# Contexts of a head in two groups of four key blocks, with a ring of six probability rows

## The reference

```
q, k, v = xh @ Wq + bq, xh @ Wk + bk, xh @ Wv + bv     # per head, xh = norm(x) as (b, s, 8, 16)
p = positions @ Wp
content = einsum('bqhd,bkhd->bhqk', q + u_bias, k)
pos_score = rel_shift(einsum('bqhd,khd->bhqk', q + v_bias, p))
attn = softmax((content + pos_score) / sqrt(128), axis=-1)
ctx = einsum('bhqk,bkhd->bqhd', attn, v)               # the "contexts" below
x = x + ctx @ Wo + bo
x = x + experts(norm(x))                               # router, top 2 of 8, gated up and down
```

## Time and profile before

| | us |
|---|---|
| median of 3 runs | 1645.3 |
| profiled execution | 1643.7 |
| its span, first to last instruction | 1641.8 |
| PE busy | 1517.0 (92%) |
| DVE busy | 1348.0 (82%) |
| ACT busy | 1094.1 (67%) |
| POOL busy | 1061.9 (65%) |

### The profile page before, as it was taken

The page is one execution under the profiler, slowest core; times in us unless marked ns, Lnnn a source line. Parts: engine busy times, 40 slices in busy tenths (PEclk is TensorE's granted clock), DMA queues, the critical chain, the costliest instruction groups (busy, mean ns, idle before and its releaser), DMA issues. The chain is left out here.

```text
span 1641.8 us, 49022 instructions
## 1 busy us (share of the span) xinstructions
PE 1517.0 (92%) x12235; PEld 1167.6 (71%) x12236; DVE 1348.0 (82%) x5147; ACT 1094.1 (67%) x2267; POOL 1061.9 (65%) x2019
## 2 busy tenths in 40 slices
PE   4799999999999999999999999999940899999997
PEld 2566676677667767767766776766530899999997
DVE  6689899889989988998898998878633688878886
ACT  3167777777777777677777777756720677777775
POOL 3177667667776766776676676655754376666766
PEclk8599999999999999999999999999975899999999
DMA  6836445544643653453364355333053244334443
GB/s 167 235 92 179 123 135 153 147 114 108 201 111 106 174 155 95 129 172 110 111 192 133 107 161 166 94 77 100 27 165 108 45 56 56 53 54 56 54 57 45
DMA packets 129820, 189.79 MB, mean 116 GB/s; under 512 B 20184, under 2 KB 93272, under 8 KB 129616
## 3 DMA queue, kind: packets, MB, share of 16 engines
q1 hardware_dynamic: 104048, 167.23, 37.2%
q0 software_dynamic: 25568, 20.14, 7.9%
HBM read 104.04 MB, written 69.96 MB: 106 GB/s over the span
## 5 line engine op out<-in xcount | busy, mean ns | idle before, releaser
L1122 DVE CUSTOM_DVE_ANT_0 junk<-pA,lmask 128x512 bf16<-128x512 f32 x1024 | 668.0, 683 | 85.0 <-PE pA L685 66.3
L1017 ACT ACTIVATE prob<-pB 128x512 f32<-128x512 f32 x384 | 229.9, 599 | 181.4 <-PE pB L704 98.5
L1653 POOL DMA_INDIRECT out<-yb,dst x142 | 231.6, 1631 | 129.6 <-ACT yb L1731 72.9
L683 PE MATMUL pA<-K,QL 96*128 96x512 f32 (+3 forms) x768 | 274.9, 359 | 12.4 <-DMA K<-split_operands 9.6
L706 PE MATMUL pB<-QL,K 97*128 97x512 f32 (+3 forms) x768 | 285.1, 372 | 1.4 <-ACT upper_diag L1017 1.2
L704 PE MATMUL pB<-QU,K 97*128 97x512 f32 (+3 forms) x640 | 265.9, 416 | 3.0 <-ACT prob L1017 1.9
L1019 ACT ACTIVATE prob<-pB 128x512 f32<-128x512 f32 x384 | 228.3, 594 | 15.1 <-PE pB L706 4.7
L685 PE MATMUL pA<-K,QU 96*128 96x512 f32 (+3 forms) x640 | 226.2, 354 | 1.2 <-DVE acc L1122 0.2
L722 PE MATMUL pC<-prob,vext 128*17 128x256 f32 x3088 | 217.0, 384 | 0.3 <-POOL prob L597 0.3
L597 POOL TENSOR_TENSOR prob<-prob,upper_diag 128x128 f32<-128x128 f32 x384 | 184.6, 481 | 32.0
L704 PEld LDWEIGHTS pB<-QU,K 97*128 97x128 f32 x640 | 120.9, 189 | 112.6 <-issue 61.8
(11 more groups left out here) (308 smaller groups left out, 3482.7 us busy)
## 6 DMA issues: line engine op xcount, KB each, us to landing
QL<-split_operands SPq DMA_DIRECT2D x64, 256.0 KB, 3.5
QU<-split_operands SPq DMA_DIRECT2D x64, 256.0 KB, 4.0
K<-split_operands SPq DMA_DIRECT2D x64, 256.0 KB, 4.3
xg<-routed_rows SPq DMA_DIRECT2D x75, 132.0 KB, 2.7
split_operands<-c_h SPq DMA_DIRECT2D x32, 256.0 KB, 5.3
split_operands<-c_l SPq DMA_DIRECT2D x32, 256.0 KB, 5.5
QL<-split_operands SPq DMA_DIRECT2D x64, 128.0 KB, 3.4
QU<-split_operands SPq DMA_DIRECT2D x64, 128.0 KB, 3.9
```

The lines of the kernel that those rows point to most:

```text
L683: mm = pe.matmul(dst[:, 0:low], QL[0:KROWS, s, q], K[0:KROWS, s, k0:k0 + low], start=True, stop=True)
L1017: act.activation(p[:, 0:HALF], pB[:, 0:HALF], ACT.Exp, scale=SCALE).then_inc(p_exp, 1)
L1122: v.tensor_tensor_reduce(out, src[:, :], lmask[:, at:at + HALF], 1.0, -3.0e38, ALU.add, ALU.max, acc[:, s, qb, n % 2:n % 2 + 1]).then_inc( ...
L1653: po.indirect_dma_start(dram["out"], bass.IndirectOffsetOnAxis(dst[k][:, a:a + 1], 0), yb[k][:, a, :], None, compute_op=ALU.add).then_inc( ...
```

## The change

The contexts of a head go in two groups of four instead of four groups of two: kb 4 to 7 of the head before in unit 1, kb 0 to 3 in unit 6. A row is so held longer, and the ring has six rows; since 8 rows a head don't divide by 6, a table FROM gives each head's first row. LATE, the count with which `pv_done` and `p_mask` start, goes from 2 to 4, and ACT waits on `pv_done` in steps of a group. The memory of the two added rows comes from the operand parts: gl now uses c's buffer. Therefore the stores of c have a semaphore of their own, `c_stored`, and from the second batch on ACT waits for them ahead of writing gl's high part (h = 3, u = 6). For the first batch gl's parts lie in rows 4 and 5 of the ring. GpSimd clears four rows ahead of the loop and not three. At the end of the last batch four contexts are left and not two.

```diff
-RING = 4
-LATE = 2
+RING = 6
+LATE = 4
-        parts = {... for n in ("c", "k", "gl", "gu")}
+        parts = {... for n in ("c", "k", "gu")}
+        parts["gl"] = parts["c"]
+        FROM = (4, 0, 2, 5, 2, 4, 0, 2)
+        def probs(h, kb):
+            return prob[(FROM[h % H] + kb % RING) % RING]
+        early_gl = (prob[4][:, :].bitcast(F32R), prob[5][:, :].bitcast(F32R))
-        PAIRS_AT = {1: (-1, 6), 4: (0, 0), 6: (0, 2), 8: (0, 4)}
+        GROUPS_AT = {1: (-1, 4), 6: (0, 0)}
-                            sp.dma_start(stored_to(...), stored_from(name, low, side)).then_inc(stored, 16)
+                            sp.dma_start(stored_to(...), stored_from(name, low, side)).then_inc(c_stored if name == "c" else stored, 16)
                             sp.wait_ge(stored, in_dram)
+                            sp.wait_ge(c_stored, c_in_dram)
-            for i in range(1, RING):
+            for i in range(4):
                 po.memset(prob[i][:, :], 1.0).then_inc(set_pool, 1)
-                        if u in PAIRS_AT:
-                            back, kb = PAIRS_AT[u]
-                            context(b, h + back, kb)
-                            context(b, h + back, kb + 1)
+                        if u in GROUPS_AT:
+                            back, from_kb = GROUPS_AT[u]
+                            for kb in range(from_kb, from_kb + NB // 2):
+                                context(b, h + back, kb)
+                if name == "gl" and half == 0 and not isinstance(nb, int):
+                    act.wait_ge(c_stored, nb * C_N)
-                            act.wait_ge(pv_done, b * (H * NB) + h * NB + u)
+                            act.wait_ge(pv_done, b * (H * NB) + h * NB + (LATE if u == 1 else 2 * LATE if u <= RING else 3 * LATE))
```

More of the change, by code:

```diff
@@ L105, in attention_phase @@
         xn = sb("xn", [P, NB, E])
-        parts = {n: (sb(n + "_h", [P, S], F32R), sb(n + "_l", [P, S], F32R)) for n in ("c", "k", "gl", "gu")}
+        parts = {n: (sb(n + "_h", [P, S], F32R), sb(n + "_l", [P, S], F32R)) for n in ("c", "k", "gu")}
+        parts["gl"] = parts["c"]
         QL, QU, K = keep["stacks"]
@@ L166, in attention_phase @@
         upper, swapped = sem("upper_form_ready"), sem("r_swapped")
-        stk, stored = [sem(f"stk{i}") for i in range(SLOTS)], sem("operands_stored")
+        stk, stored, c_stored = [sem(f"stk{i}") for i in range(SLOTS)], sem("operands_stored"), sem("content_operands_stored")
         d_r, d_big, set_r = sem("router_in"), sem("experts_in"), sem("set_router")
@@ L249, in attention_phase @@
         PLACES = {"c": ((0, 0), (1, 0)), "k": ((2, 0),), "gl": ((0, 1),), "gu": ((1, 1),)}
-        ST_N = 16 * 4 * sum(len(p) for p in PLACES.values())
+        ST_N, C_N = 16 * 4 * sum(len(p) for p in PLACES.values()), 16 * 4 * len(PLACES["c"])
         STORE_AT = {2: ("c",), 3: ("k",), 4: ("gl", "gu")}
         READY = {"c": 2, "k": 4, "gl": 7, "gu": 8}
-        PAIRS_AT = {1: (-1, 6), 4: (0, 0), 6: (0, 2), 8: (0, 4)}
+        GROUPS_AT = {1: (-1, 4), 6: (0, 0)}
         FOUR, SIDE = H // 2, P // 2
@@ L259, in stored_to, with stored_from @@
             return dram["operands"][bass.ds(nb % 2, 1), op, FOUR * side:FOUR * side + FOUR, 2 * low + row, :, :].rearrange("o h d s -> (o d) h s")
-        def stored_from(name, low, side):
-            return parts[name][low][SIDE * side:SIDE * side + SIDE, :].bitcast(F32)
-        DVE_SET, DVE_BIAS, POOL_SET = 14, 12, 15
+        def stored_from(name, low, side, early=False):
+            return (early_gl if early and name == "gl" else parts[name])[low][SIDE * side:SIDE * side + SIDE, :].bitcast(F32)
+        DVE_SET, DVE_BIAS, POOL_SET = 14, 12, 16
         D_W, D_CST = 16 * 8, 16 * 5
@@ L325, in store @@
                         for side in range(2):
-                            sp.dma_start(stored_to(nb, op, low, row, side), stored_from(name, low, side)).then_inc(stored, 16)
+                            sp.dma_start(stored_to(nb, op, low, row, side), stored_from(name, low, side)).then_inc(c_stored if name == "c" else stored, 16)
             def store_side(name, side):
@@ L330, in store_side @@
                     for low in range(2):
-                        sp.dma_start(stored_to(0, op, low, row, side), stored_from(name, low, side)).then_inc(first_stored[side], 16)
+                        sp.dma_start(stored_to(0, op, low, row, side), stored_from(name, low, side, True)).then_inc(first_stored[side], 16)
             sp.sem_inc(d_x2, 16)
@@ L368, in batch @@
                         sp.dma_start(xt[:, :, :], dram["x"][bass.ds((b + 2) % B, 1)].rearrange("o (t p) e -> p (o t) e", p=P)).then_inc(d_x, 16)
-                    through, in_dram = known(sp, HPB * (b * (H * S2U) + h * S2U) + 1), known(sp, (b + 1) * ST_N)
+                    through, in_dram, c_in_dram = (known(sp, n) for n in (HPB * (b * (H * S2U) + h * S2U) + 1, (b + 1) * (ST_N - C_N), (b + 1) * C_N))
                     sp.wait_ge(set_dve, DVE_SET)
@@ L419, in _ @@
                 sp.wait_ge(mrow_in[i], 4 * B * 32)
-            sp.wait_ge(stored, (B - 1) * ST_N)
+            sp.wait_ge(stored, (B - 1) * (ST_N - C_N))
+            sp.wait_ge(c_stored, (B - 1) * C_N)
             sp.wait_ge(swapped, B * 64)
@@ L451, in _ @@
             po.memset(vext[:, :, :, :], 0.0).then_inc(set_pool, 1)
-            for i in range(1, RING):
+            for i in range(4):
                 po.memset(prob[i][:, :], 1.0).then_inc(set_pool, 1)
             po.memset(mhalf[:, :], -0.5).then_inc(set_pool, 1)
-            po.wait_ge(set_pool, 9)
+            po.wait_ge(set_pool, 10)
             po.affine_select(out=ident[:, :], in_=ident[:, :], compare_op=ALU.not_equal, fill=1.0, base=0,
@@ L589, in batch @@
                             if kb > 0:
-                                po.memset(prob[kb % RING][0:1, P * kb - 1:P * kb], 0.0)
-                            p = prob[kb % RING][:, P * kb:P * kb + P]
+                                po.memset(probs(h, kb)[0:1, P * kb - 1:P * kb], 0.0)
+                            p = probs(h, kb)[:, P * kb:P * kb + P]
                             po.affine_select(out=p, in_=p, compare_op=ALU.is_ge, fill=0.0, base=0,
@@ L721, in context @@
                 for strip in range(STRIPS):
-                    mm = pe.matmul(pC[VW * strip:VW * strip + D + 1, :], vext[:, kb, h % H, :], prob[kb % RING][:, quarter * strip:quarter * strip + quarter],
+                    mm = pe.matmul(pC[VW * strip:VW * strip + D + 1, :], vext[:, kb, h % H, :], probs(h, kb)[:, quarter * strip:quarter * strip + quarter],
                                    start=(kb == 0), stop=(kb == NB - 1), skip_group_check=True)
@@ L937, in high @@
                 cut = slice(HALF * half, HALF * half + HALF)
-                act.activation(parts[name][0][:, cut], src[:, cut], ACT.Copy).then_inc(hi_done, 1)
+                if name == "gl" and half == 0 and not isinstance(nb, int):
+                    act.wait_ge(c_stored, nb * C_N)
+                dst = early_gl if name == "gl" and isinstance(nb, int) else parts[name]
+                act.activation(dst[0][:, cut], src[:, cut], ACT.Copy).then_inc(hi_done, 1)
             def upper_high(nb, half, src):
@@ L1106, in low @@
                 v.wait_ge(hi_done, nb * HI_N + n + 1)
-                v.tensor_tensor(parts[name][1][:, cut], src, parts[name][0][:, cut].bitcast(F32), ALU.subtract).then_inc(low_done, 1)
+                high, dst = early_gl if name == "gl" and isinstance(nb, int) else parts[name]
+                v.tensor_tensor(dst[:, cut], src, high[:, cut].bitcast(F32), ALU.subtract).then_inc(low_done, 1)
             def super_out(src, done):
```

2 lines of the change are left out of this document (1 added, 1 removed).

## The result

The changed kernel takes 1715.37 us (median of 4 runs, 1714.85 to 1715.67) against 1643.97 (1641.35 to 1646.98) of the kernel before in the same comparison: a ratio of 1.0425, 95% interval 1.0396 to 1.0453. Forecast were 1656 us, range 1630 to 1682. The direction was right, the size was not, and the range didn't hold it.

What follows compares the result with a forecast made beforehand. Three close limits: PE in units 1, 4, 6, 8, the PE-ACT round trip elsewhere, and DVE. Per head -0.23 + 0.35 + 0.05 = +0.17, times 64 +11, with prologue +12: 1643.7 + 12 = 1656 us, range 1630 to 1682.

Steps and rivals of the forecast that it cites:

- units 1 and 6, two contexts more each: Units 1 and 6 each stream two more contexts on PE: 2 x 0.88 = 1.76 us a head.
- unit 4: Without contexts, unit 4 drops from 2.41 to the PE-ACT round-trip floor of 1.34: 1.07 us saved a head.
- unit 8: Without contexts, unit 8 drops from 2.26 to the floor of 1.34: 0.92 us saved a head.
- unit 5: ACT's extras from unit 4 delay unit 5's first exponential: +0.30 us a head, mostly heads 5 and 7.
- unit 0: ACT's extras after unit 8 delay unit 0, in head 0 behind head 7's two jobs: +0.05 us a head.
- VectorE: DVE idles at the longer groups, but has about room: +0.05 us a head for heads 0 and 2; bound 1.76.
- clock: No term for a change of PE's granted clock in the main loop, read as 0.99, its 2.4 GHz level.
- The switches: Two groups replace four pairs: in and out cost about 0.2 us a group, saving 0.4 us of PE a head.
- ScalarE's side jobs: ACT's extras of units 4 and 8 lose the contexts' cover, lengthening units 5 and 0: +0.35 us a head.
- DVE starves: Rival: PE delivers no piece for some 2.6 us around each group, then DVE paces short units; 1675 to 1694 us; chance 0.17.
- Edits costed at nothing: ACT's new waits on pv_done and c's stores, ring order, split store semaphore, POOL's masks, last head's pair: no cost.
- Prologue: One more POOL memset of 1024 columns ahead of the loop delays DVE's first xn and PE: +0.9 us once.

Runs made afterwards that it cites:

- run 6: Changed kernel plus idle matmuls where TensorE waits in heads 0, 3, 5 and 7, and in units 2 and 3 of head 6: 1688.01 us.
- run 1: Changed kernel with its buffers, ring of six and wait for c's stores, but context pairs at units 1, 4, 6 and 8 as before: 1644.01 us.
- run 3: Changed kernel's buffers and ring, but only unit 4 loses its contexts: four at unit 6, pairs at units 8 and 1: 1684.14 us.
- run 4: Changed kernel with ACT's side jobs at units 4 and 8 cut from 512 columns to 16: 1717.76 us.
- run 7: Changed kernel with ACT's side jobs and DVE's big ones at units 4 and 8 cut to 16 columns or one head: 1684.94 us.
- run 9: Changed kernel with the big side jobs of ACT and DVE cut to 16 columns or one head in every unit: 1667.01 us.

## Why the prediction was wrong, step by step

Per head, forecast against the undisturbed lengths after (for unit 6 of head 3, where the clock fell in every batch, the length in run 6):

| term | forecast | measured |
|---|---|---|
| units 1 and 6, two contexts more each | +0.88, +0.88 | +0.83, +0.96 |
| unit 4 | -1.07 | -1.09 |
| unit 8 | -0.92 | -1.04 |
| unit 5 | +0.30 | +0.52 |
| unit 0 | +0.05 | +0.24 |
| other units, and what varies between batches | 0 | +0.03 |
| VectorE | +0.05 | in units 5, 0 and 6 |
| clock | none | +0.67 |
| sum | +0.17 | +1.12 |

- *The switches.* Right: 1.85 for a group, units 4 and 8 at 1.33 and 1.27. A pair taken from unit 4 gave 1.09, a pair added to unit 6 of heads 1, 4, 5 and 6 took 0.86 or 0.87, so in and out are 0.2 a group, as the forecast read from its rows. Its estimate from the Trainium skill, page "TensorE: Matmul & The Clock Gate", section "Single matmul latency", 0.33, is not borne out.
- *ScalarE's side jobs.* Right in its mechanism and, in three places, to 0.05 us: unit 5 of head 5 2.43 (forecast 2.44) and of head 7 2.25 (2.25), unit 0 of head 0 2.09 to 2.19 (2.10 to 2.15). Unit 5 of heads 1, 4 and 6, forecast at nothing, grew by 0.20, 0.09 and 0.09. In the timeline the exponential stands right behind L990, as the forecast said:

```profile
779.97 0.77 ACT L989 ACTIVATE rq<-pM,r_cols 128x512 f32<-128x512 f32 x1
780.63 0.78 ACT L990 ACTIVATE rq<-pM,r_cols 128x512 f32<-128x512 f32 x1
781.29 0.60 ACT L1030 ACTIVATE prob<-pB 128x512 f32<-128x512 f32 x1
```

- *VectorE.* The step that failed first. The forecast compared DVE's idle time per head (1.8 us) with what the longer groups take (1.76), and put +0.05 in heads 0 and 2. It also placed DVE's side jobs in units 1, 4, 6 and 8 alone. The tables and the timeline have them elsewhere too: statistics of the router's rows in unit 2 of head 2 (0.86 us for four), a low part (0.76) in its unit 3. DVE lags by three pieces at most, so what counts is the backlog in a given unit. Heads 2 and 3 have it at unit 5 (+0.82 and +1.08, forecast +0.2 each), heads 0, 2 and 7 at unit 6 (+1.26, +1.00, +1.10 where +0.88 is streaming). Heads 1 and 7 had +0.54 and +0.77 in unit 0, where PE's small pieces wait for what DVE got at unit 8 or just ahead. Its rival "DVE starves" had the right engine and the wrong place: DVE is not late because it starves at the groups, but because units without contexts leave it no time. Its price, a sixth of 1.76, 0.3 a head, is close to what the undisturbed heads show beyond the forecast (0.45 less 0.17, 0.28), by luck, since it was worked out from the idle time at the groups.
- *The clock.* The step that was missing. The forecast read 0.99 in the earlier trace rows, the trace of one fall, and carried it over without saying so; no term and no rival had it, though 0.67 a head is more than all the others together. The forecast knew that PE would wait in units 5, and took the wait at its own length. The falls cost about 37 us besides, nearly half of the 82 us that they last.
- *Edits costed at nothing.* Right, by run 1; ahead of gl's high part (now named c_h) ACT does not wait: 598.95, right behind the job at 598.47.
- *Prologue.* 0.9 forecast, 1.65 in the profiled execution after, 1.4 in run 1. But in all eleven profiled kernels with the added memset the loop opens between 76.4 and 80.2, in the three without it between 78.3 and 78.9, so no single pair of executions can show this term.

With 0.45 a head for all 64 heads and no fall of the clock the forecast's sum would have come to 1643.7 + 29 + 2, about 1675, inside the range. The clock took it outside.

## What to carry to other kernels

A long stretch of matmuls in the middle of a pipeline is also the time in which the other engines catch up; merging two such stretches saves switches and takes that time away from the places where the backlog stands, which an idle time per head doesn't show. Price it unit by unit, from the record of the engine that lags. And where PE runs at its full clock without a gap, treat new waits of 0.6 to 1.1 us within a unit as more than themselves: in these traces they were often followed by half the clock in what came next, and useless matmuls in the wait brought it back.

## What was not expected of the hardware

- The clock fell behind 0.6 to 1.1 us of waiting in one unit, and at head 6 without any wait, behind units of small matmuls (this in the kernel before too). The same wait in the same unit was followed by a fall in some batches and not in others (unit 6 of head 3 in run 3: in two of the first seven batches).
- In the changed kernel with ACT's side jobs cut (runs 4, 7 and 9) one small operation of DVE takes 1.47 us in 6, 5 and 7 of the first seven batches, where it takes 0.22 in the kernels before and after. In run 9 it starts 0.28 ahead of a mask of POOL over 1024 columns and ends with it (782.98 against 782.90):

```profile
781.51 1.47 DVE L1284 TENSOR_TENSOR both<-oh 128x64 bf16<-128x64 f32 x1
```

```profile
781.79 1.11 POOL L595 TENSOR_SCALAR_AFFINE_SELECT upper_diag<-upper_diag 128x1024 f32<-128x1024 f32 x1
```

PE's piece "ranks" waits for it, and in 16 of these 18 batches the clock falls behind that. The Trainium skill, page "SBUF — State Buffer", section "Who interferes with whom", says that DVE and GpSimd share one pair of ports as an exclusive lock, and that the one that issues second is blocked. The trace agrees in that the two end within 0.1 us of each other in all 18, but by the records DVE started first. In the three batches of runs 4 and 7 where the operation takes 0.22, the mask starts 0.57 behind it. But the distance doesn't decide it: in three batches of the changed kernel and in all seven of run 6 the mask starts 0.28 behind it as well, and it takes 0.22. No run here took the mask away, and what makes the operation long stays open. It raises head 7, and with it the whole time, in runs 4, 7 and 9.
